# Spreading the residual updates of one token tile over all eight experts instead of the first four

## The reference, cut to what matters

```
x = x + 0.5 * ffn(layernorm(x))
x = x + attention(layernorm(x))        # 16 heads, window of 128 on each side, rotary
x = x + 0.5 * ffn(layernorm(x))

def ffn(x):                            # x: (2, 8192, 1024), 8 experts
    chosen = argmax(x @ gate_w.T)      # one expert for each token
    return x + sum over e of onehot[e] * (x @ expert_w[e].T)   # each (1024, 1024)
```

## Time and profile before

| what | value |
|---|---|
| time, median of 3 runs | 2643.68 us (2641.61 to 2644.29) |
| the profiled execution, its own time | 2651.38 us |
| span of its slowest core (core 2) | 2649.8 us |
| PE busy | 2080.1 us, 79% of the span |
| DVE busy | 849.9 us, 32% |
| ACT busy | 447.3 us, 17% |
| POOL busy | 379.3 us, 14% |
| PE in the FFN matmuls (`pdf`) | 1065.9 us busy, 206.3 us idle just before them |

### The profile page before, as it was taken

The page is one execution under the profiler, slowest core; times in us unless marked ns, Lnnn a source line. Parts: engine busy times, 40 slices in busy tenths (PEclk is TensorE's granted clock), DMA queues, the critical chain, the costliest instruction groups (busy, mean ns, idle before and its releaser), DMA issues.

```text
span 2649.8 us, 27883 instructions; the slowest of 8 cores (2618.1 to 2649.8 us)
## 1 busy us (share of the span) xinstructions
PE 2080.1 (79%) x9872; PEld 1039.3 (39%) x9872; DVE 849.9 (32%) x1704; ACT 447.3 (17%) x1059; POOL 379.3 (14%) x511
## 2 busy tenths in 40 slices
PE   1686777989897479968977996898686979797963
PEld 0572223434345324423433442343662434343452
DVE  1203113232323344245234424524113232324232
ACT  1300000000000104612740561275200000000000
POOL 0000114141414200000000000000000141414142
PEclk9657988989898686578568657857557989898987
DMA  7004994535345653002001100100004545353446
GB/s 212 1 0 87 199 195 135 170 108 161 107 150 164 134 130 94 1 32 76 27 32 64 38 1 32 64 1 32 1 0 112 146 126 158 118 161 110 151 144 213
DMA packets 78117, 257.60 MB, mean 97 GB/s; under 512 B 9232, under 2 KB 20496, under 8 KB 73888
## 3 DMA queue, kind: packets, MB, share of 16 engines
q0 software_dynamic: 57648, 203.28, 27.9%
q1 hardware_dynamic: 20336, 52.55, 6.5%
HBM read 249.27 MB, written 33.63 MB: 107 GB/s over the span
## 4 chain that ended last, share of the span: by engine, by line
PE 72%; DMA 10%; DVE 9%; issue 3%; ACT 2%; POOL 2%; SPq 1%; DVEq 0%; POOLq 0%; ACTq 0%
PE pdf L93 34%; PE pss L93 11%; PE pq L93 5%; PE pgf L93 5%; PE pspt L98 4%; PE pv L93 3%; DMA webuff<-wexpT 3%; DMA webuff<-wexp_bf 3%; PE pbf L93 3%; PE pso L93 2%; DMA wexp_bf<-webuff 2%; SPq L150 1%; PE pba L93 1%; DVE uscrf L104 1%; POOL uscrf L104 1%
## 5 line engine op out<-in xcount | busy, mean ns | idle before, releaser
L93 PE MATMUL pdf<-lmbuff,webuff 128*128 128x512 bf16 (+1 forms) x5120 | 1065.9, 373 | 206.3 <-DVE lmbuff L104 104.2
L93 PEld LDWEIGHTS pdf<-lmbuff,webuff 128*128 128x128 bf16 x5120 | 513.6, 101 | 758.5 <-issue 289.8
L104 DVE TENSOR_TENSOR lmbuff<-xcf,mkbuff 128x1024 bf16<-128x1024 bf16 (+1 forms) x320 | 217.0, 686 | 766.8 <-PE pdf L93 752.0
L150 POOL DMA_DIRECT2D webuff<-wexp_bf x288 | 153.3, 533 | 1080.6 <-PE pdf L93 924.3
L125 ACT CAST ev8f<-pdf 128x1024 bf16<-128x1024 f32 (+1 forms) x20 | 17.6, 930 | 1500.8 <-PE pdf L93 1500.8
L111 DVE TENSOR_SCALAR pn_bf_at<-p_at,rc_at 128x384 bf16<-128x384 f32 x256 | 96.0, 417 | 239.8 <-PE pspt L98 238.2
L141 ACT ACTIVATE p_at<-pss,negc_at 128x384 f32<-128x384 f32 x256 | 147.8, 590 | 36.1 <-PE pss L93 35.5
L93 PE MATMUL pss<-biasq_sb,idb 128*128 128x384 bf16 x256 | 128.5, 502 | 15.4 <-DVE k_sb_at L104 15.4
L93 PE MATMUL pss<-k_sb_at,q_sb_at 64*128 64x384 bf16 x256 | 127.7, 499 | 0.0
L93 PE MATMUL pgf<-gwT_sb,x_sb 128*128 128x8 f32 x576 | 123.2, 362 | 0.0
L93 PEld LDWEIGHTS pgf<-gwT_sb,x_sb 128*128 128x128 f32 x576 | 123.0, 333 | 0.0
(11 more groups left out here) (120 smaller groups left out, 1547.1 us busy)
## 6 DMA issues: line engine op xcount, KB each, us to landing
webuff<-wexp_bf POOLq DMA_DIRECT2D x288, 512.0 KB, 4.5
webuff<-wexpT POOLq DMA_DIRECT2D x32, 512.0 KB, 11.8
wexp_bf<-webuff SPq DMA_DIRECT2D x32, 512.0 KB, 9.3
wbufA_at<-wqkv_bf POOLq DMA_DIRECT2D x6, 2048.0 KB, 9.7
wbufB_at<-wqkv_bf POOLq DMA_DIRECT2D x6, 2048.0 KB, 9.0
x_sb<-xT SPq DMA_DIRECT2D x8, 1152.0 KB
mkbuff<-onehot_sc SPq DMA_DIRECT2D x64, 128.0 KB, 7.5
outT<-x_sb SPq DMA_DIRECT2D x8, 1024.0 KB, 12.1
```

Of the source, the lines that this page charges most:

```text
L93: E.matmul(a, b, c, start=st, stop=sp, tile_position=tp),
L104: eng, lambda E, o=out, x=a0, y=a1, op=op: E.tensor_tensor(o, x, y, op),
L150: eng, lambda E, o=out, i=in_: E.dma_start(o, i), inc=sem, n=16)
```

## The change

Ahead of each expert the kernel before took one update from the list, and for experts e0 to e3 a second one. So e0 carried d0 and d1, e1 carried d2 and d3 (DVE), e2 carried d4 and d5, and e3 carried d6 and d7 (POOL). The second one is taken out. Each expert now carries one update: e0 to e3 carry d0 to d3, e4 to e7 carry d4 to d7. No instruction is added or removed in any engine's list, and no instruction goes to another engine.

```diff
                 for e in range(8):
                     if pending:
                         cc, eng = pending.pop(0)()
                         ph2[eng] = cc
-                    if e < 4 and pending:
-                        cc, eng = pending.pop(0)()
-                        ph2[eng] = cc
                     if e == 5 and ti + 1 < len(tcs):
```

## The result

| | before | after |
|---|---|---|
| time, median of 8 runs each | 2644.25 us (2641.61 to 2646.93) | 2580.01 us (2574.95 to 2584.18) |
| ratio | | 0.9755, 95% interval 0.9744 to 0.9765 |
| the profiled execution | 2651.38 us | 2581.33 us |
| span of its slowest core | 2649.8 us (core 2) | 2579.7 us (core 6) |

What follows compares the result with a forecast made beforehand. The prediction took PE, waiting for DVE's `lmbuf` products and POOL's weight loads, as the bound. Savings of 25.5 + 4.2 + 11.8 + 11 = 52.5 us gave 2591 us for the median, range 2560 to 2614.

Steps and rivals of the forecast that it cites:

- Start of a tile: Wait ahead of a tile's first product: one update fewer, gap 9.65 to 6.46 us, 25.5 us saved in all.
- DVE's d1 to d3, cost zero: Ahead of the second to fourth expert: DVE's updates of 3.2 us each stay hidden by about 10 us of matmuls.
- e2 and e3 of the wide tiles: Tiles 1 to 3, no update on POOL there: gaps and slow restarts go, 44.4 us over six tiles.
- e4 and e5, cost zero, and d7 hidden: Wide tiles: one POOL update delays loads without making PE wait; d7 runs in the shadow of e6's gap.
- Rival C: Late single load ahead of e4 and e5 opens its own gap: slower, 2661 us at a 10 us landing; chance 4%.
- e6: Wide tiles: `gen_xc` holds POOL's d6 for 4.25 us; tiles 1 and 2 save only 4.2 us, tile 3 11.8 us.
- I + 11.2: Forecast issue of e6's first load, I being when POOL issues the load of the previous expert's last piece.
- Tile 3: At e6, `gen_xc` covers only 256 tokens: gap of 0.8 us without clock loss, 5.9 us saved, twice.
- Tile 4: 256-token tile, one update at each of the last four experts: two gaps with slow clock, 5.5 us saved per FFN.
- A: At e6, `gen_xc` does not hold POOL up: 80.9 us saved, 2563 us; chance 20%.
- B: POOL's cost only moves to e6, tile 4 saves nothing: 2616 us; chance 14%.
- D: Nothing changes, because the start of the tile waits for something that DVE's list hides; chance 2%.

Runs made afterwards that it cites:

- POOL's part alone: Against the kernel before: only POOL's updates spread out, one ahead of each of the last four experts, DVE's stay in pairs; 2608.1 us, ratio 0.9843.

## Why the prediction was right, and where it was off

*Start of a tile.* Right: 9.65 to 6.46 us in every wide tile from 1 on, on every core (9.38 to 6.20 in tile 4). The slow clock behind it stayed, as said: 384 matmuls take 84.3 to 86.0 us after it.

*DVE's d1 to d3, cost zero.* Right: no gap stands in the six experts behind the start.

*e2 and e3 of the wide tiles.* Right that both gap and slow restart go. The sum of 44.4 us was too large: I had read the slowest core alone, whose six gaps are 4.6 us long on average and lose 2.8 us each. Over all cores of the kernel before the gap is 3.9 us and the loss 2.0 us on average, and 8 of the 48 lose nothing (gaps of 3.4 to 3.8 us with 83.0 to 83.2 us behind them). That is 35.5 us in the six tiles, 9 less.

*e4 and e5, cost zero, and d7 hidden.* Right: on 8 cores no gap stands ahead of e4 or e5 of a wide tile, and one of 0.31 us ahead of e7. Rival C did not show.

*e6.* The mechanism was right: `gen_xc`, with two inputs in SBUF, held POOL's instruction for 4.0 us. The rule of the Trainium skill ("SBUF — State Buffer", section "Who interferes with whom"), that the two exclude each other, holds here for a long instruction too: POOL's 1.15 us took 5.16. The order was not as forecast. `gen_xc` is listed first, as said, but POOL's first instruction ran undisturbed and `gen_xc` waited 1.33 us; DVE's d2 beside POOL's d4 shows the same (2.02 us instead of 0.69, listed 0.18 us ahead of POOL's 1.28). By these starts it is not always the one listed later that waits. So POOL's second instruction took the 5 us that the forecast had seen in the first, and the loads went out at I + 10.43 instead of I + 11.2.

The size of this term was off: "in tiles 1 and 2 the gap of e2 comes back at e6, 1.04 us shorter ... four tiles save only 4.2 us". By the four gaps of the earlier trace rows that charges 3.9 us of gap (4.98 - 1.04) and 2.8 us of clock in each of four tiles, 6.7 us. Over 8 cores, tiles 1 and 2 and both FFNs the gap is 2.35 us on average (32 gaps), and only 3 of the 32 restarts were slow, with 1.7 us each: 2.5 us a tile, 4.2 us less, 17 us in four tiles. The kernel with POOL's part alone agrees (2608 us, and not the 2617 us that a gap of 2.8 us with 2.8 us of clock would give), and the lengthened d6 shows that the same place does cost clock once its gap is long. The bounds of the e6 term ("nothing held to everything returning") contained it; what they did not name is that gap and clock do not come back together.

The total came out closer than its terms, and that is luck: the 17 us too much at e6 stand against the 9 us too much at e2. With some 1 us each in tile 3, in tile 4 and of clock at the starts this gives 11 us, of the 11.7 between 52.5 and the 64.2 us that the stretches give by means.

*Tile 3.* A gap of 0.8 us without loss was forecast; 12 of 16 have none to speak of and four have 0.57 to 1.46 us. Right.

*Tile 4.* 5.5 us in each FFN were forecast, 6.0 and 6.8 measured by medians, 5.8 and 6.1 by means, with gaps of 3.7 and 3.0 us ahead of e4 and e6 on the slowest core in the place of 9.5 and 2.6:

```profile
809.83 8.81 PE L93 MATMUL pdf<-lmbuff,webuff 128*128 128x256 bf16 x64 [3.69 <-DMA webuff<-wexp_bf]
...
830.63 10.72 PE L93 MATMUL pdf<-lmbuff,webuff 128*128 128x256 bf16 x80 [2.96 <-DMA webuff<-wexp_bf]
```

*Rivals.* A (no hold) is out by the 5.16 us. B (everything returns at e6) is out by the gaps' length: 2.35 us and 3 slow restarts of 32, where e2 had 3.9 us and 40 of 48. C is out, no gap stood ahead of e4 and e5, and so is D, the start of the tile shrank by the whole 3.19 us.

## What to carry to other kernels

In a kernel whose engines run in program order, side work costs what stands behind it in the list: ask of each piece which load or operand is queued behind it and how far ahead that one is needed, and give each such stretch one piece that fits its slack. When a stall gets shorter, price the stall and the slow clock behind it apart, from gaps of the new length, and on all cores: here the gap went from 3.9 to 2.35 us and the clock's cost from 2.0 to 0.2 us. Before moving work in time, look what the other engine does there, if the two are seen to hold each other up; two cheap pieces at the same place made the only gap that was left.

## What the runs showed of the hardware that I had not expected

- Ahead of e6, slow restarts set in gradually with the length of the gap, and not at one length: none of 99 below 2.4 us, 17 of 43 from 2.4 to 3.6 us, 49 of 51 above.
- The same length does not cost the same at every place: behind the 3.21 us gap at a tile's start 22 of 48 tiles lost clock in one kernel, and 34 and 35 of 48 in two others, and behind 1.48 and 0.54 us 17 of 84 did.
- POOL's issue of a DMA (0.53 us) is not stretched while `gen_xc` runs on DVE (485.81 beside 482.46 to 486.88 has 0.53 us), while POOL's tensor_tensor is held until it ends.
- When two engines take turns, both lose: with d2 on DVE and d4 on POOL at the same time, both took about 1.5 us per instruction, and DVE's update became twice as long (6.9 us from 419.29 to 426.2 instead of 3.2).
